# Weighted layer-norm products made beside the squares, and scaling moved to GpSimd, in a four-layer graph network on one Trainium2 core

## The reference

```python
x = layernorm(x + L0(x))   # L0: 8-head attention with an edge-weight bias matrix (bias = -1e9, 0 on the diagonal,
                           #     edge_weight at [dst, src]); h = LN(x + attn@Wo.T + bo)*g1+beta1;
                           #     h = LN(h + h@W1.T + b1)*g2+beta2
x = layernorm(x + L1(x))   # L1: relu(D^-1/2 A D^-1/2 (x @ W) + b), D and A with self loops
x = layernorm(x + L2(x))   # L2: h = x@self_W + self_b + mean over edges of (x@rel_W[type] + rel_b[type]);
                           #     x1 = LN(x + h)*g+b; out = LN(x1 + gelu(x1@W1+b1)@W2 + b2)*g+b
x = layernorm(x + L3(x))   # L3: 8-head attention over the edges, o = a@Wo; x1 = LN(x + o)*g+b;
                           #     out = LN(x1 + relu(x1@W1+b1)@W2 + b2)*g+b
```

## Time and profile before

| | before |
|---|---|
| three runs, us | 543.94, 542.71, 540.62 (median 542.71) |
| the profiled execution, us | 543.4 |
| its span from first to last instruction, us | 541.7 |
| TensorE matmul busy, us | 508.9 (94%) |
| VectorE busy, us | 387.2 (71%) |
| ScalarE busy, us | 228.8 (42%) |
| GpSimd busy, us | 268.8 (50%) |
| mean granted TensorE clock | 0.981 of full |

### The profile page before, as it was taken

One profiled execution on the slowest core, in us unless ns is written; L12 is line 12 of the kernel. 1 busy time (PEld: TensorE's weight loads), 2 busy tenths in 40 slices (PEclk: granted clock), 3 DMA queues, 4 the chain that ended last, 5 costly groups with the idle time before them and its releaser, 6 DMA issues.

```text
span 541.7 us, 7832 instructions
## 1 busy us (share of the span) xinstructions
PE 508.9 (94%) x2483; PEld 348.3 (64%) x2498; DVE 387.2 (71%) x982; ACT 228.8 (42%) x478; POOL 268.8 (50%) x270
## 2 busy tenths in 40 slices
PE   8989999999998999998999999998999999899982
PEld 3434444445886555885778888888887786564781
DVE  6999989999975786878544853845437625776576
ACT  2102460004515775667451243424525126785455
POOL 5477777767407887302541544613441753867001
PEclk9999999999997999999999999999999998999987
DMA  6922400000497320143553665322463753100002
GB/s 193 353 87 80 116 21 0 0 0 2 125 321 221 91 60 21 41 136 98 175 161 79 178 198 149 93 78 79 119 195 101 223 160 87 51 1 0 2 0 77
DMA packets 32409, 56.48 MB, mean 104 GB/s; under 512 B 5152, under 2 KB 8686, under 8 KB 31864
## 3 DMA queue, kind: packets, MB, share of 16 engines
q1 hardware_dynamic: 19420, 31.61, 19.7%
q0 software_dynamic: 11728, 18.92, 12.2%
q10 hardware_dynamic: 1228, 5.54, 2.8%
HBM read 51.79 MB, written 4.26 MB: 103 GB/s over the span
## 4 chain that ended last, share of the span: by engine, by line
PE 57%; DVE 18%; DMA 7%; issue 6%; ACT 5%; POOL 5%; DVEq 1%; SPq 0%; POOLq 0%; ACTq 0%
PE bank L573 10%; PE bank L550 8%; PE bank L552 8%; PE bank L551 8%; PE bank L679 5%; PE bank L666 3%; DMA wraw<-w_o 3%; PE bank L770 3%; PE bank L769 3%; DVE hot L1282 3%; PE bank L657 2%; DVE hot L1281 2%; DVE eq L1263 2%; POOL edge_bias L434 2%; POOL wl L390 2%
## 5 line engine op out<-in xcount | busy, mean ns | idle before, releaser
L390 POOL TENSOR_TENSOR wl<-wraw,wh 128x512 fp32r<-128x512 f32 (+1 forms) x78 | 101.0, 1310 | 106.5 <-DMA wraw<-w_o 20.1
L573 PE MATMUL bank<-hot 128*128 128x512 bf16 x514 | 114.3, 379 | 3.7 <-DVE hot L1282 2.8
L573 PEld LDWEIGHTS bank<-hot 128*128 128x128 bf16 x528 | 51.2, 98 | 66.8 <-DVE hot L1282 6.0
L434 POOL DMA_INDIRECT edge_bias<-ew,cell_at x68 | 73.1, 1074 | 37.9 <-issue 18.4
L550 PE MATMUL bank<-wh,tl 128*128 128x512 f32 x176 | 69.5, 395 | 0.5 <-DVE tl L1190 0.5
L552 PE MATMUL bank<-wh,th 128*128 128x512 f32 x176 | 68.8, 391 | 0.0
L551 PE MATMUL bank<-wl,th 128*128 128x512 f32 x176 | 68.7, 390 | 0.0
L1282 DVE TENSOR_SCALAR hot<-iota,pair_dst,digit 128x1024 bf16<-128x1024 f16 x68 | 42.4, 624 | 0.0
L941 ACT ACTIVATE sp<-sp,peak 128x512 f32<-128x512 f32 x44 | 31.8, 722 | 24.1 <-DVE peak L1467 23.8
L1263 DVE SCALAR_TENSOR_TENSOR eq<-keyb,key,later 128x384 f16<-128x384 f16 (+1 forms) x68 | 39.9, 608 | 0.0
L550 PEld LDWEIGHTS bank<-wh,tl 128*128 128x128 f32 x176 | 33.1, 188 | 8.7 <-issue 2.1
(11 more groups left out here) (240 smaller groups left out, 1048.9 us busy)
## 6 DMA issues: line engine op xcount, KB each, us to landing
wraw<-w SPq DMA_DIRECT2D x26, 256.0 KB
wh<-w POOLq DMA_DIRECT2D x6, 1024.0 KB, 6.3
keyb<-edge_keys ACTq DMA_DIRECT2D x4, 1088.0 KB, 10.0
wh<-w_rel POOLq DMA_DIRECT2D x4, 1024.0 KB, 5.9
wraw<-w_rel SPq DMA_DIRECT2D x16, 256.0 KB
wraw<-w_qkv SPq DMA_DIRECT2D x8, 256.0 KB
wh<-w_o POOLq DMA_DIRECT2D x2, 1024.0 KB, 7.7
count_rows<-counts SPq DMA_DIRECT2D x1, 2048.0 KB, 12.5
```

Of the source, the lines that this page charges most:

```text
L390: pool.tensor_tensor(wl[n % WSLOTS][:, k, 0:width], wraw[:, q % 3, 0:width], wh[n % WSLOTS][:, k, 0:width], ALU.subtract).then_inc(s["w_lo ...
L434: pool.indirect_dma_start(out=bias_dram, out_offset=bass.IndirectOffsetOnAxis(ap=cell_at[:, c:c + 1], axis=0), in_=ew[:, c:c + 1], in_offs ...
L573: mm = pe.matmul(ps(name)[:], hot[:, slot, 0, i * P:(i + 1) * P], hot[:, slot, 1 + kind, :], start=False, stop=last, skip_group_check=True)
```

## The change

- Weighted norms: the product (h + neg) * gain becomes a step of its own, `centred`, written to x instead of h and placed in front of the wait for ScalarE's root. `affine` and `affine_and_add` keep one step each. Since x held the residual, `centred` stands behind a wait for all of `res_ready`, which moves ahead for norms 0, 4 and 7.
- Norm 2: GpSimd normalises the four tiles (behind `cast(6)`, in front of `cast(7)`), ScalarE only scales by the degree, VectorE makes the reciprocal alone (`inverse_root`). `scaled_low(3)` goes ahead of `choose_rows`, and `low(6)` and `low(7)` wait for `rows_chosen`.
- Attention 0: GpSimd's `low(3)` moves from in front of the scaling into it, so twelve low parts stand behind items 3, 5, 7, 10, 12 and so on to 28; `cast(5)` is issued behind item 11; the wait for `call_summed` goes.
- Masks and the rounded identity are built by GpSimd behind its four early subtractions instead of by VectorE.
- Norms 4 and 7: the transposes of tiles stand earlier in TensorE's order, and some copies earlier in ScalarE's and VectorE's. ScalarE casts one early weight quarter (`weight_high(6)`) later.

```diff
@@ GpSimd @@
+                    if a == 0 and m == 11:
+                        cast(5)
...
+            pool.wait_ge(s["ld_ident"], 16)
+            pool.tensor_scalar(ident_r[:], ident[:], 1.0, None, ALU.mult).then_inc(s["masks_ready"], 1)
+            pool.wait_ge(s["masks_ready"], 1)
+            for n in range(4):
+                link(pool.tensor_scalar(masks[:, n, :], ident[:], 0.0, None, ALU.mult))
+            for n in range(4):
+                rows_ = slice(32 * n, 32 * n + 2)
+                pool.tensor_scalar(masks[rows_, n, :], ident[rows_, :], 0.0, 1.0, ALU.mult, ALU.add).then_inc(s["masks_ready"], 1)
+                pool.wait_ge(s["masks_ready"], n + 2)
...
             cast(3)
-            pool.wait_ge(s["call_summed"], 2)
-            low(3)
             cast(4)
-            cast(5)
-            scale_rows(0, 0, None, {4 + 3 * j: (n, [f]) for j, (n, f) in enumerate((n, f) for n in (4, 5) for f in range(K))})
+            scale_rows(0, 0, None, {3 + 7 * j // 3: (n, [f]) for j, (n, f) in enumerate((n, f) for n in (3, 4, 5) for f in range(K))})
...
+            def normalise(L, i):
+                c = 4 * L + i
+                pool.wait_ge(shifted[L], i + 1)
+                pool.tensor_scalar(x[:, i, :], h[:, i, :], neg[:, c:c + 1], rstd[:, c:c + 1], ALU.add, ALU.mult).then_inc(normed[L], 1)
+            for i in range(T):
+                normalise(2, i)
             cast(7)
-            pool.wait_ge(normed[2], T)
+            pool.wait_ge(s["rows_chosen"], 2)
             low(6)
             low(7)
@@ TensorE @@
-            pe.wait_ge(s["masks_ready"], 4)
+            pe.wait_ge(s["masks_ready"], 5)
...
+                    if i >= 2 and r == 2:
+                        turn(2, h, 4, i - 2)
...
-                if i >= 2:
-                    turn(2, h, 4, i - 2)
...
-                    if i == 3 and k == 3:
+                    if i == 3 and k == 2:
                         turn(4, h, 7, 1)
@@ ScalarE @@
-            for q in range(4, 7):
+            for q in range(4, 6):
                 weight_high(q)
...
+            weight_high(6)
...
-                normalise(2, i)
+                act.wait_ge(normed[2], i + 1)
...
             turned(4, 0)
+            turned(4, 1)
             deviation(7, 2, h[:, 2, :])
-            turned(4, 1)
@@ VectorE @@
+            def centred(L, i, gain):
+                c = 4 * L + i
+                dve.wait_ge(summed[L], i + 1)
+                link(dve.scalar_tensor_tensor(out=x[:, i, :], in0=h[:, i, :], scalar=neg[:, c:c + 1], in1=par[:, gain, :],
+                                              op0=ALU.add, op1=ALU.mult))
...
-                link(dve.scalar_tensor_tensor(out=h[:, i, :], in0=h[:, i, :], scalar=nm, in1=par[:, gain, :], op0=ALU.add, op1=ALU.mult))
-                dve.scalar_tensor_tensor(out=h[:, i, :], in0=h[:, i, :], scalar=r, in1=par[:, add, :], op0=ALU.mult, op1=ALU.add)\
+                dve.scalar_tensor_tensor(out=h[:, i, :], in0=x[:, i, :], scalar=r, in1=par[:, add, :], op0=ALU.mult, op1=ALU.add)\
...
             centre(0, 0, ("o0", 0), x[:, 0, :])
+            dve.wait_ge(s["res_ready"], T)
+            centred(0, 0, 2)
             call_low(2)
             call_low(3)
             centre(0, 1, ("o0", 1), x[:, 1, :])
-            affine(0, 0, 2, 3)
+            centred(0, 1, 2)
+            affine(0, 0, 3)
...
-            affine_and_add(1, 1, 4)
+            affine_and_add(1, 1)
             centre(1, 2, ("f0", 2), h[:, 2, :])
             scaled_low(0)
-            shift_of(2, 1)
-            affine_and_add(1, 2, 4)
+            centred(1, 2, 4)
+            inverse_root(2, 1)
+            affine_and_add(1, 2)
...
-            shift_of(2, 3)
+            inverse_root(2, 3)
+            scaled_low(3)
             choose_rows()
-            scaled_low(3)
...
+            dve.wait_ge(s["res_ready"], 2 * T)
+            for i in range(T):
+                if i >= 2:
+                    turned(2, i - 2)
+                spread_over(i)
+                centred(4, i, 2)
+                affine(4, i, 3)
...
+            dve.wait_ge(s["res_ready"], 3 * T)
+            for i in range(T):
+                centre(7, i, ("o3", i), x[:, i, :])
+                if i == 2:
+                    turned(4, 0)
+                    turned(4, 1)
+                centred(7, i, 2)
+                affine(7, i, 3)
...
             centre(8, 0, ("f3", 0), h[:, 0, :])
+            centred(8, 0, 0)
             centre(8, 1, ("f3", 1), h[:, 1, :])
-            affine_and_add(8, 0, 0)
+            affine_and_add(8, 0)
             half_low(1, 0)
             half_low(1, 1)
-            affine_and_add(8, 1, 0)
+            centred(8, 1, 0)
+            affine_and_add(8, 1)
```

More of the change, by code:

```diff
@@ L501, in _ @@
             for i in range(T - 2):
-                c = 4 * 9 + i
-                pool.wait_ge(shifted[9], i + 1)
-                pool.tensor_scalar(x[:, i, :], h[:, i, :], neg[:, c:c + 1], rstd[:, c:c + 1], ALU.add, ALU.mult).then_inc(normed[9], 1)
+                normalise(9, i)
         @block.tensor
@@ L1217, in reciprocal_of, with affine, affine_and_add @@
                 return neg[:, c:c + 1], rstd[:, c:c + 1]
-            def affine(L, i, gain, add):
+            def centred(L, i, gain):
[3 more added lines that the diff above has]
+                                              op0=ALU.add, op1=ALU.mult))
+            def affine(L, i, add):
                 nm, r = reciprocal_of(L, i)
-                link(dve.scalar_tensor_tensor(out=h[:, i, :], in0=h[:, i, :], scalar=nm, in1=par[:, gain, :], op0=ALU.add, op1=ALU.mult))
-                dve.scalar_tensor_tensor(out=h[:, i, :], in0=h[:, i, :], scalar=r, in1=par[:, add, :], op0=ALU.mult, op1=ALU.add)\
+                dve.scalar_tensor_tensor(out=h[:, i, :], in0=x[:, i, :], scalar=r, in1=par[:, add, :], op0=ALU.mult, op1=ALU.add)\
                     .then_inc(normed[L], 1)
-            def affine_and_add(L, i, gain):
+            def affine_and_add(L, i):
                 nm, r = reciprocal_of(L, i)
                 c = 4 * (L + 1) + i
-                link(dve.scalar_tensor_tensor(out=h[:, i, :], in0=h[:, i, :], scalar=nm, in1=par[:, gain, :], op0=ALU.add, op1=ALU.mult))
-                link(dve.scalar_tensor_tensor(out=h[:, i, :], in0=h[:, i, :], scalar=r, in1=y[:, i, :], op0=ALU.mult, op1=ALU.add,
+                link(dve.scalar_tensor_tensor(out=h[:, i, :], in0=x[:, i, :], scalar=r, in1=y[:, i, :], op0=ALU.mult, op1=ALU.add,
                                               accum_out=total_z[:, c:c + 1]))
@@ L1320, in bias_rows @@
                                          op1=ALU.add).then_inc(s["add2_ready"], 1)
[L1322 to L1327, removed]
             dve.wait_ge(s["ld_ew"], 16)
@@ L1527, in _ @@
             centre(0, 1, ("o0", 1), x[:, 1, :])
-            affine(0, 0, 2, 3)
+            centred(0, 1, 2)
+            affine(0, 0, 3)
             centre(0, 2, ("o0", 2), x[:, 2, :])
-            affine(0, 1, 2, 3)
+            centred(0, 2, 2)
+            affine(0, 1, 3)
             turned(0, 0)
             centre(0, 3, ("o0", 3), x[:, 3, :])
-            affine(0, 2, 2, 3)
+            centred(0, 3, 2)
+            affine(0, 2, 3)
             turned(0, 1)
-            affine(0, 3, 2, 3)
+            affine(0, 3, 3)
             dve.wait_ge(ld_par[4], 16)
-            dve.wait_ge(s["res_ready"], T)
             centre(1, 0, ("f0", 0), h[:, 0, :])
+            centred(1, 0, 4)
             turned(0, 2)
@@ L1541, in _ @@
             dve.reciprocal(deg[:, 3, :], deg[:, 2, :]).then_inc(s["dinv"], 1)
-            affine_and_add(1, 0, 4)
+            affine_and_add(1, 0)
             centre(1, 1, ("f0", 1), h[:, 1, :])
+            centred(1, 1, 4)
             turned(0, 3)
-            shift_of(2, 0)
+            inverse_root(2, 0)
             def scaled_low(i):
@@ L1551, in scaled_low @@
                                          op0=ALU.mult, op1=ALU.subtract).then_inc(s["rowl_ready"], 1)
-            affine_and_add(1, 1, 4)
+            affine_and_add(1, 1)
             centre(1, 2, ("f0", 2), h[:, 2, :])
             scaled_low(0)
-            shift_of(2, 1)
-            affine_and_add(1, 2, 4)
+            centred(1, 2, 4)
+            inverse_root(2, 1)
+            affine_and_add(1, 2)
             centre(1, 3, ("f0", 3), h[:, 3, :])
             scaled_low(1)
-            shift_of(2, 2)
-            affine_and_add(1, 3, 4)
+            centred(1, 3, 4)
+            inverse_root(2, 2)
+            affine_and_add(1, 3)
             def choose_rows():
@@ L1713, in _ @@
             dve.wait_ge(ld_par[0], 32)
-            dve.wait_ge(s["res_ready"], 2 * T)
             centre(5, 0, ("f2", 0), h[:, 0, :])
+            centred(5, 0, 0)
             centre(5, 1, ("f2", 1), h[:, 1, :])
-            affine_and_add(5, 0, 0)
-            affine_and_add(5, 1, 0)
+            centred(5, 1, 0)
+            affine_and_add(5, 0)
+            affine_and_add(5, 1)
             standard(6, 0)
```

(6 more changed lines are left out.)

29 lines of the change are left out of this document (4 added, 25 removed).

## The result

The changed kernel takes 533.71 us (median of 6 runs, 531.65 to 534.6), the kernel before 540.6 in the same set: 6.9 between the medians. The ratio over all runs is 0.9852, 95% interval 0.9824 to 0.988, which is 8.0 us. The forecast was 534.5. In the experiments the same two kernels stood at 530.03 and 539.83, ratio 0.9823 (0.9795 to 0.9852), 9.5 us. The profiled execution took 533.68 with a span of 531.8, 9.9 under the span of before.

What follows compares the result with a forecast made beforehand. TensorE works nearly all the time, so only its gaps can be saved. The nine terms sum to 8.2 us, which against a median of 542.7 gives 534.5 us, range 531.0 to 540.0.

Steps and rivals of the forecast that it cites:

- B: Start of the first attention: dissolving GpSimd's block of four low parts makes it like the second attention, gain 1.8 us.
- E: Norms 1 and 2: earlier product, scaling on GpSimd, and low part ahead of the choice of rows gain 3.1 us.
- A: First 30 us: masks and rounded identity move to GpSimd, so chunk 12 waits less, gain 0.7 us.
- G: Norms 5 and 6: VectorE some 0.8 us earlier, but TensorE's waits there are small, gain 0.3 us.
- I: Norms 8 and 9: tile 0's product delays tile 1's eviction by 0.2, loss 0.1 us.
- C: End of the first attention: a low part behind row 28 delays the last scaled rows, loss 0.4 us.
- D: Norm 0: the reversed order makes tile 0's last step late for TensorE, loss 0.7 us.
- F: Norm 4: earlier transposes of tile 1 remove the wait at layer 2's MLP, gain 1.6 us.
- H: Norm 7: earlier transposes and copies remove the wait at layer 3's MLP, gain 1.9 us; low end 0.4.
- Rival 1: Shared port: VectorE stalls beside GpSimd's early operations and norm 2 scaling, 2.6 us lost, 537.1 us; chance 0.15.
- Rival 2: Half clock at layer 3's MLP or VectorE's queue in norms 1 and 2 takes 3.0 us, 537.5 us; chance 0.15.
- Rival 4: First attention: GpSimd's scaling of rows becomes the bound, costing up to 10.2 us, 546.1 us; chance 0.04.

Runs made afterwards that it cites:

- second profiles: The kernel before and the changed kernel, each run and profiled again unchanged: ratio 1.0013 for the kernel before; 530.03 us, ratio 0.9823 for the changed kernel.
- experiment 2: Changed kernel with the block of four low parts put back in front of the first attention: ratio 0.9819 to the kernel before.
- Experiments 8: Changed kernel with three orders mended (norm 0's last step, layer 3's last transposes, the first attention's low parts): 530.8 us, ratio 0.9833 to the kernel before.
- 11: Changed kernel with two orders mended, norm 0's last step and the first attention's low parts: 529.42 us, ratio 0.9804 to the kernel before.
- experiments 9: Changed kernel with the choice of rows again ahead of the last scaled low part and GpSimd's low parts not waiting for the choice: ratio 0.994 to the kernel before.
- 10: Changed kernel with the choice again ahead of the last scaled low part, but GpSimd's low parts waiting for both: 533.71 us, ratio 0.9841 to the kernel before.
- experiment 12: Changed kernel with norm 5's weighted product behind the reciprocal again: 531.92 us, ratio 0.9849 to the kernel before.

## Why the prediction was right, and where it was not

The total was right with terms that were mostly right and two (B and E) that stood on the wrong reason. That 8.2 met 8.0 so closely is partly luck: between the second profiles B gave 1.8 less than forecast, and A, G and I together 2.0 more. Measured from the table's "again" columns, unless another source is named:

- **A** 0.7 forecast; 1.1 at chunk 12, 1.5 to 1.7 at the first score (0.85 between the first profiles). The forecast paid half of the meetings with GpSimd at 0.36; VectorE paid 0.03 each. The first score differs by more than that between executions of the same instructions, so only the 1.1 is shown.
- **B** 1.8 forecast; 2.65 in the first profiles, 0 between the second ones, 0.92 in experiment 2. The failed step is "the second attention has no such block" as the reason for 19.7 against 17.84. I didn't ask when the block starts: its idle time ended with a DMA, and the second profile has it start 4.4 earlier. Nor did I look at the clock: 6.8 us of the first attention's 19.7 ran at half clock, and 3.4 of the second's 17.84. The part's real worth seems to be that it lets A's gain through. The sign that I named, peak to product near 18, came out as 17.0, as in the second profile of before.
- **C** -0.4 and **D** -0.7 forecast; -0.40 and -0.74. Both were walks through one queue. Experiments 8 and 11 show that both losses were avoidable.
- **E** 3.1 forecast; 3.18, the sum right and two of its three reasons sized wrongly. The product is worth 1.4 (less than two of its 0.75: not every link is on the path), ScalarE's relief 0, and the parting of choice and low parts the rest, 1.8 (by subtraction). Undone it costs even 4.0, as another operation of the choice meets the low parts then. I had seen 1.82 against 0.74 and put the gain down to order and neighbour together; it was the neighbour alone (experiments 9 and 10).
- **F** 1.6 forecast; 1.79, and 1.75 when undone. **H** 1.9 forecast; 1.90 up to the MLP and 0.35 behind it. Undone together they give back 4.2. The low end of H didn't come: with the gap its half clock vanished.
- **G** 0.3 forecast; 1.14. I read only the waits (0.3 and less) and took 0.8 of VectorE's time as cover; experiment 12 shows 0.94 of it on the path.
- **I** -0.1 forecast; +0.25. The last norms' products are made ahead too; no run takes this apart.
- **Not in the forecast**: the way from the last group of scaled rows to layer 2's self sums. At full clock it took 15.63 before and 15.70 to 16.75 in eleven profiles of the changed kernel and its versions. GpSimd's low parts now come later and meet a two-input operation of norm 3, which took 0.69 in both profiles of before, 0.97 after and 1.67 after again: the sooner behind the start of a low part it begins (0.87 and 0.17), the longer it takes. No run tests it, but 0.1 to 1.1 is lost there, and when the low part begins hangs on a DMA.

```profile
257.02 2.99 POOL L390 TENSOR_TENSOR wl<-wraw,wh 128x512 fp32r<-128x512 f32 x2 [1.54 <-DMA wraw<-w_self]
257.19 1.67 DVE L1649 SCALAR_TENSOR_TENSOR h<-h,x 128x512 f32<-128x512 f32 x1
```

The terms from A to I add up to 9.0 (1.5 for A, 0 for B). The other 1.8 of the 10.8 between the second spans (539.05 and 528.24) are 0.82 of half clock in the second attention of before, and 0.99 in the stage just named. There half clock cost the second profile of before some 1.5 (VectorE's first eviction comes 7.40 behind the last group, against 5.87 in the first profile), and the changed kernel lost 0.9 of its own. Ratios over all runs give 8.0 and 9.5 us, less than the spans, since the profiled executions of before are on the slow side of its runs.

In the prediction's working two sums are off: the high ends of the terms add up to 12.2, not 12.1, and A and E at their ends with the spread of 1.6 make 3.0, not 3.5, so the lower bound would be 531.5. Neither changes the outcome.

Rival 1, the port: its price for VectorE's products didn't appear, and the same contention decided E in another place. Rival 2, the clock: at layer 3's MLP it was not the new waits that brought it, but the old one; in the second attention it took 1.6 from one profile of the changed kernel and nothing from the other. Rival 3, late weights: no wait for a weight's low part appeared. Rival 4: waits for GpSimd's rows are 0.5 in two, as in the second profile of before. What would have shown the prediction wrong was a product of 1.3 beside GpSimd's scaling; the longest was 0.95.

## What to carry to other kernels

Part a small operation from another engine's two-tensor work before you count its order: 4 us hung on a 16-column operation that stood next to three low parts, and nothing on the order. Follow the moved work to where it stands now: the low parts that left the choice met norm 3. A wait on TensorE can be worth more than its length if the clock falls behind it, and nothing if it covers another wait, so follow the way between two fixed instructions and not the waits. Take a second profile of the kernel before: a term that rests on when a DMA landed, or on a stretch of low clock, isn't one of the kernel.

## What the runs showed of the hardware

- Beside GpSimd's two-tensor low parts VectorE stood still for the whole of three of them (4.46 us for 0.23). A comparison near the start of the kernel before did the same (4.70 for 0.34). Beside its masks and scalings VectorE lost next to nothing in most places (0.37 for 0.34, 0.77 for 0.75), 0.2 in the tail of every changed profile (0.94 or 0.95 for 0.75) and 0.37 in the choice of experiments 9 and 10 (0.60 for 0.23), and GpSimd lost 0.3 to 0.5 each (0.84 for 0.54, 1.27 for 0.77).
- The granted clock fell to 0.5 behind the 1.8 to 2.2 us gap at layer 3's MLP in three profiles of three. Near the gap of 2.0 in front of the last scaled rows it fell in one profile of before and not in the other. In the second attention, with gaps of 0.8 and less, it fell in 8 of 14 profiles, in one of the changed kernel and not in the other: 20.23 and 18.66 us for the same stage. What decides there stays open.
- The first 160 us differ by up to 3.6 us between executions with the same instructions (160.22 to 163.85 at the first score). That wasn't traced further.
